# Ranks of the second half: a count from the removal phase in place of four matmuls per piece

## The reference

```python
def step(carry, n):
    row = jnp.take(carry, n, axis=0)
    nbi = row.astype(jnp.int32)
    num = jnp.sum(nbi)
    sf = jnp.where(num > T_DIL, (num + K_DIL - 1) // K_DIL, 1)
    rank = jnp.cumsum(nbi)
    rm = row & (rank % sf == 0)
    valid = (mask_b[n] != 0) & (num > 1)
    rm = jnp.where(valid, rm, False)
    keep = ~rm
    carry = carry.at[n].set(row & keep)
    carry = carry.at[:, n].set(carry[:, n] & keep)
    return (carry, None)
```

## Time and profile before

| | |
|---|---|
| median of 3 runs | 1330.38 us (1329.29 to 1331.5) |
| profiled execution, its own time | 1330.83 us |
| its span, first to last instruction | 1329.1 us |
| mean granted TensorE clock | 0.960 of full speed |
| TensorE busy | 1204.1 us, 91% of the span |
| VectorE / ScalarE busy | 791.4 us, 60% / 595.4 us, 45% |

### The profile page before, as it was taken

The page is one execution under the profiler, slowest core; times in us unless marked ns, Lnnn a source line. Parts: engine busy times, 40 slices in busy tenths (PEclk is TensorE's granted clock), DMA queues, the critical chain, the costliest instruction groups (busy, mean ns, idle before and its releaser), DMA issues. The chain is left out here.

```text
span 1329.1 us, 29132 instructions
## 1 busy us (share of the span) xinstructions
PE 1204.1 (91%) x10849; PEld 1033.7 (78%) x10849; DVE 791.4 (60%) x2835; ACT 595.4 (45%) x1519; POOL 114.8 (9%) x129
## 2 busy tenths in 40 slices
PE   4999799988598999998989999899998899998998
PEld 4999666655377787777869999799998599996554
DVE  5999455566655655565542544444536466676983
ACT  4888246766644454454322333404343432332441
POOL 4432000000000000000000000023323010110000
PEclk9999889987599999999989999999999899999999
DMA  9977011111235665446324756036757335462931
GB/s 323 314 262 278 2 23 27 28 19 22 73 155 222 229 248 200 183 191 244 126 89 174 301 219 274 1 120 246 282 211 285 127 127 207 186 241 84 407 96 48
DMA packets 105523, 229.06 MB, mean 172 GB/s; under 512 B 34529, under 2 KB 53153, under 8 KB 105377
## 3 DMA queue, kind: packets, MB, share of 16 engines
q1 hardware_dynamic: 104656, 227.07, 46.3%
q10 hardware_dynamic: 720, 0.07, 0.0%
HBM read 185.70 MB, written 37.75 MB: 168 GB/s over the span
## 5 line engine op out<-in xcount | busy, mean ns | idle before, releaser
L1371 PE MATMUL lay_acc<-lay_z,k_otheradj 128*128 128x128 f32 x1024 | 118.3, 277 | 0.0
L1371 PEld LDWEIGHTS lay_acc<-lay_z,k_otheradj 128*128 128x128 f32 x1024 | 117.1, 194 | 0.0
L1371 PE MATMUL lay_acc<-lay_z,k_keepadj 128*128 128x128 f32 x1024 | 117.0, 275 | 0.0
L1371 PEld LDWEIGHTS lay_acc<-lay_z,k_keepadj 128*128 128x128 f32 x1024 | 115.6, 192 | 0.0
L1419 ACT ACTIVATE lay_junk<-lay_o 128x128 bf16<-128x128 f32 x128 | 37.7, 295 | 124.2 <-DVEq L1508 123.9
L1102 ACT ACTIVATE fuse_dist<-fuse_prank,k_kb 128x512 f16<-128x512 f32 (+2 forms) x96 | 55.2, 575 | 76.1 <-PE fuse_prank L993 72.9
L1485 DVE TENSOR_TENSOR lay_o<-lay_ring,k_vec 128x512 f32<-128x512 f32 x32 | 22.1, 692 | 106.2 <-PE lay_ring L1364 106.2
L1465 POOL TENSOR_TENSOR lay_bl<-k_vec,k_mask 128x256 f32<-128x256 f32 x32 | 21.2, 664 | 617.9 <-DVEq L1498 614.2
L993 PE MATMUL fuse_prank<-k_fore,k_T 128*128 128x128 fp8e5 (+3 forms) x416 | 63.3, 291 | 10.5 <-PEq L140 7.2
L333 PE MATMUL att_acc<-att_rhs,att_adjT 128*128 128x130 f32 x512 | 59.8, 280 | 13.9 <-POOLq L285 12.3
L333 PEld LDWEIGHTS att_acc<-att_rhs,att_adjT 128*128 128x128 f32 x512 | 59.1, 195 | 14.4 <-POOLq L285 12.4
(11 more groups left out here) (288 smaller groups left out, 2722.4 us busy)
## 6 DMA issues: line engine op xcount, KB each, us to landing
k_keepadj<-in_adj_cols SPq DMA_DIRECT2D x28, 1024.0 KB, 9.1
k_keepadj<-keptT SPq DMA_DIRECT2D x12, 2048.0 KB, 10.8
k_otheradj<-keptT SPq DMA_DIRECT2D x12, 2048.0 KB, 11.5
att_adjT<-in_adj_cols SPq DMA_DIRECT2D x16, 1024.0 KB, 8.2
k_otheradj<-in_adj_cols SPq DMA_DIRECT2D x16, 1024.0 KB, 10.5
keptT<-k_keepadj SPq DMA_DIRECT2D x16, 1024.0 KB, 4.6
keptT<-k_otheradj SPq DMA_DIRECT2D x16, 1024.0 KB, 4.3
lay_rowf<-in_adj_rows SPq DMA_DIRECT2D x32, 512.0 KB, 14.6
```

The lines of the kernel that those rows point to most:

```text
L1371: mm = t.matmul(acc[i % 2][k][:, ib % HB, :], adjT[i % 2][:, jb, ib * P:(ib + 1) * P], zz[i % 2][:, jb, :], start=(jb == 0), stop=(jb == N ...
```

## The change

Pieces of the second half (lo = 512) no longer include the row blocks 0 to 3: their first row block is 4. What those four blocks would have added is one number per row and graph. It is counted in the removal phase: in `far_counts`, for blocks 0 to 3, four further one-column matmuls per graph add into four further columns of `pl`. At the head of iteration 5 VectorE copies these into `lowcount`; before the last `staying` it adds them to the biases of row blocks 4 to 7 and writes `kbhigh`. `distances` takes its bias from `kbhigh` for pieces of the second half and from `kb` for the others.

```diff
@@ removal_phase
+    LOW = NB // 2
+        lowcount = s.sb("lowcount", [P, LOW, B], F32)
@@ far_counts
                         for jb in range(nb + 2, NB):
                             add(pl[:, jb, b:b + 1], T8[:, b, nb, jb * P:(jb + 1) * P], K["ones8"][:, 0:1])
+                        if nb < LOW:
+                            for jb in range(LOW, NB):
+                                add(pl[:, NB + jb - LOW, b:b + 1], T8[:, b, nb, jb * P:(jb + 1) * P], K["ones8"][:, 0:1])
@@ VectorE, head of an iteration
                         v.tensor_copy(base, pl[:, 0, :])
+                    if nb == LOW + 1:
+                        v.tensor_copy(lowcount[:], pl[:, NB:NB + LOW, :])
                     dve.drain()
                     limits(nb)
@@ VectorE, after the last iteration
                     dve.drain().then_inc(far_params, 1)
+                high = K["kb"][:].rearrange("p (b t) -> p t b", t=NB)[:, LOW:NB, :]
+                v.tensor_tensor(K["kbhigh"][:], high, lowcount[:], ALU.add)
                 staying(NB - 1, range(B))
@@ fuse_phase, ranks
-                        last_jb = min(nb, (hi - 1) // P)
-                        for jb in range(last_jb + 1):
+                        first_jb, last_jb = lo // P, min(nb, (hi - 1) // P)
+                        for jb in range(first_jb, last_jb + 1):
                             a = max(jb * P, lo)
                             mm = t.matmul(prank[n % NR][:, a - lo:hi - lo], T8[:, b, jb, nb * P:(nb + 1) * P],
-                                          K["fore8"][:, a - jb * P:hi - jb * P], start=(jb == 0), stop=(jb == last_jb))
+                                          K["fore8"][:, a - jb * P:hi - jb * P], start=(jb == first_jb), stop=(jb == last_jb))
@@ fuse_phase, distances
-                        a.activation(dist[n % NR][:, 0:hi - lo], prank[n % NR][:, 0:hi - lo], ACT.Abs, bias=K["kb"][:, tile:tile + 1])
+                        bias = K["kb"][:, tile:tile + 1] if lo == 0 else K["kbhigh"][:, nb - NB // 2, b:b + 1]
+                        a.activation(dist[n % NR][:, 0:hi - lo], prank[n % NR][:, 0:hi - lo], ACT.Abs, bias=bias)
@@ build_program
+        resident("kbhigh", [P, z.NB // 2, B])
```

## The result

The changed kernel takes 1322.12 us (median of 4 runs, 1320.47 to 1323.47) against 1330.14 us of the kernel before (4 runs): ratio 0.9938, 95% interval 0.9921 to 0.9955. The forecast was 1320.9 us with a range of 1316.5 to 1325.5. The profiled execution took 1321.10 us, its span is 1319.4 us.

The account below looks back on a forecast made before the run. TensorE, busy 91% of the span, was taken as the bound where no wait for ScalarE or VectorE follows. Gains of 12.0 us (9.1 + 1.95 + 0.9) less 2.5 us costs took 1330.38 to 1320.9 us, range 1316.5 to 1325.5.

Parts of the forecast that it names:

- Price of the columns: Removed rank matmuls in stages 4 to 7: about 0.424 ns per column, 2.17 us per graph, 17.4 us in all.
- Stages 4 and 5 swallowed behind ScalarE: Graphs 1 to 6: the 0.22 and 0.43 us removed there gain nothing, since TensorE still waits for ScalarE.
- Stages 6 and 7 whole: Graphs 1 to 6: all 1.52 us removed per graph count, 9.1 us; with stage 5, graph 0 gains 1.95 us.
- Lead-in: Fuse phase before graph 0's first masks: 0.9 us of the 2.17 us removed is gained.
- Counts at 25 ns, 24 of 32 on the path: Removal phase: added one-column matmuls cost 0.6 us per block, 2.4 us for four; the last eight are hidden.
- The copy: VectorE's copy of 32 elements from PSUM at iteration 5 of removal costs 0.1 us.
- The addition: Making `kbhigh` before the last `staying`, while VectorE waits for ScalarE's first distance, costs nothing, at most 0.2 us.
- The 81 ns: Rule against the forecast: 96 exposed counts cost 7.8 us, removed matmuls return about 8 us, so time stays unchanged.
- The clock: Rival, 15%: changed timing turns a 4 us half-clock stretch in the removal phase, 2 us either way: 1319 or 1323.
- all columns come off: Rival, 8%: stages 4 and 5 and the lead-in count too, the whole 17.4 us, giving 1315.5 us.
- the period is held elsewhere: Rival, 6%: VectorE or transfers fill in stages 6 and 7's gain; 2.9 us or nothing gained, 1330.0 to 1332.9.
- the counts cost their duration: Rival, 3%: each extra count costs 164 ns on the removal path, giving 1334.2 us.

Follow-up runs that it names:

- the split kernels: Changed kernel and kernel before, each with ScalarE's eight norm activations split into two halves of four: 1312.32 us and 1326.61 us.
- experiment 2: Kernel before with the extra counts, copy and addition added, but all rank matmuls and the old bias kept: 1335.85 us, ratio 1.0032.
- experiment 1: Changed kernel without the 128 extra one-column counts in the removal phase: 1316.31 us, ratio 0.9891.
- 4: Changed kernel, but only the pieces of row blocks 6 and 7 leave out the first four row blocks: 1319.59 us, ratio 0.9918.
- 7: Changed kernel with ScalarE's eight norm activations split into two halves, in stages 3 and 4: 1312.32 us, ratio 0.9867.
- 12: Changed kernel with the norm activations split and 14 matmuls without use before the lead-in: 1313.28 us, ratio 0.9864.
- experiment 11: Changed kernel with 14 matmuls without use (512 columns) on TensorE at the end of the removal phase: 1320.27 us, ratio 0.9929.

## Why the prediction was right

- **Price of the columns.** 0.424 ns each from start to start: confirmed by the split kernels' 2.25 us per graph for 2.17. The durations of the form table would have given about double.
- **Stages 4 and 5 swallowed behind ScalarE.** Shown: the two waits grew by 0.22 and 0.35 us; cutting there alone brought 0.5 to 0.8 us of 4.5; with the activations split, the columns counted.
- **Stages 6 and 7 whole.** Shown: 9.45 us for six graphs against 9.1, graph 0 1.95 against 1.95, and the cut there alone gives 10.9 of the whole cut's 11.4 us. Graphs 1 to 6 take 226.57 us with it and 226.52 with the whole cut, so stages 4 and 5 give nothing there, as said; 0.3 of the 9.45 us are there without any cut (235.66 us in experiment 2, 235.97 before).
- **Lead-in.** Right as a mechanism (0.92 us where the clock is as before, 14.65 - 13.67 = 0.98 where both kernels have the counts), but the changed kernel's lead-in is no shorter than the one before. What the sum lacks is a cost: about 1 us in this stretch that comes with the counts, since the clock is full only at 365.6 us, 5.9 us after the first rank, and before at 361.9, 3.5 us after it. The replay from the earlier trace rows took the clock as given.
- **Counts at 25 ns, 24 of 32 on the path.** Shown by rounds 2 and 3: 2.35 us for 2.4, the last eight hidden. The copy cost 0.1 us or less: iteration 5's round 0 goes from 3.85 to 3.95 us. The addition took 0.21 us in VectorE's wait for ScalarE, as said. The duration as a price (164 ns) is refuted here. The 81 ns that the Trainium skill (TensorE: Matmul & The Clock Gate, Back-to-back issue gap) gives for a stream of weight load and matmul is its figure for 128 columns, and the prediction put it on matmuls of one column. For 1 to 64 columns the table of the same section has an issue floor of about 25 ns, and with that the trace agrees. For 512 columns it gives 131 ns in such a stream, and there the trace does not agree: 0.424 ns per column is 217 ns.
- **The clock.** Listed as a rival at 2 us either way; in fact it came together with the forecast's other terms. In iteration 4's round 1 the changed kernel gains 0.46 us, since its clock is full where it was at 0.66 before; in iteration 1's round 0 it loses 0.52 us. Over the removal phase such shifts nearly cancel (+2.11 against the rounds' +2.35); between experiment 1 and the changed kernel they make about 3.1 of the 3.6 us in the lead-in and the rest of the kernel.

The window of iteration 4's round 1 before the change:

```profile
...
276.00:281.00 5.00, 5.00 (x33) 2.67 (x30) 3.94 (x20) 3.57 (x7) 0.00 (x0) 0.66 0.34 52
...
```

And after it:

```profile
...
278.00:283.00 5.00, 4.14 (x52) 2.69 (x50) 3.73 (x22) 3.92 (x7) 0.00 (x0) 1.00 0.41 64
...
```

The forecast of 1320.9 us lies 1.2 us under the median. The two profiled executions are 9.7 us apart, close to the 9.5 of the sum, and there the lead-in's missing 0.9 us is made up by three things: 0.4 us less in the removal phase than forecast, 0.35 more from graphs 1 to 6, and 0.7 us at the start of the kernel, which no term of the sum foresaw. The last is luck. Of the 1.2 us, 1.0 is the distance of the profiled run (1321.10) from the median of its four.

The rivals "all columns come off", "the period is held elsewhere" and "the counts cost their duration" are out: 1322.1 us against 1315.5, at least 1330.0 and 1334.2. The rest of the kernel, unchanged, takes 656.7 to 660.8 us in these profiles. In the pairs set beside each other (1 and the changed kernel, 4 and the changed kernel, 7 and 12) 2.1 of 2.6, 1.2 of 1.7 and all of 2.8 us lie in stretches of which one kernel has more at a clock of 0.50. What stays open is the remainder, and why a half-clock stretch falls where it does.

## What to carry to other kernels

Where a matmul is taken out matters more than how many: a stream's columns are worth their start-to-start price only behind the last wait of the loop's period, and a cut ahead of a wait is worth nothing until that wait is moved. Here moving it (half of ScalarE's norm behind the distances) was worth 8.2 us in graphs 0 to 6, of which 4.4 are columns that it had swallowed. And when a change is worth a fraction of a percent, compare stretches of the trace and not totals: the clock's half-rate stretches shift with everything that is moved.

## What the runs showed of the hardware

- A one-column matmul with its own 128 x 128 weights costs 25 ns in a stream, though weight load and matmul are recorded with about 97 and 164 ns: seven of the eight rounds 2 and 3 grew by 0.30 us for 12, the eighth by 0.25. At half clock it is hardly more: in the kernel before, 24 of them go from 298.72 to 299.36 us, 27 ns each, in a stretch (298 to 300) with a granted clock of 0.50.
- Code that starts 1.4 us later can meet full clock 3.7 us later: the clock is full from 361.9 us before and from 365.6 us after. A second profile of the changed kernel shows the same pattern (both have a mean clock of 0.959; the other runs of this kernel lie between 0.957 and 0.961). And a stretch brought to full clock early can fall back to half in the next (experiment 11: 1.88 us won, 1.63 lost).
- The same instructions can differ by more than the change under study: 44.4 us at a mean clock of 1.00 and 47.4 at 0.93 between the same two instructions (7 and 12). The kernel that leaves out less work (4) had a median 2.5 us below that of the one that leaves out more, with 0.5 us more in the stretch that was changed; the intervals of their ratios overlap.
